# One bias row-add for each PSUM bank instead of one for each product, in a four-layer network on one core

## The chip, the cores and the metric

One Trainium2 chip, one core. The metric is the device time of one execution in microseconds (us), the median over the runs shown. Busy times, waits and the order of the work come from one profiled execution of the same program.

## What is computed

Four layers, each a feed-forward block, an attention block and the feed-forward block again, on x of shape (4, 512, 128) in float32. The parts that the change meets are the linear maps with a bias:

```python
q = (q_in @ Wq.T + bq)            # layer 1 feed-forward: k and v likewise
attn_out = ctx @ out_proj_w.T + out_proj_b
gates = softmax(x1 @ gate_w.T + gate_b)
logits = x @ router_w + router_b  # layer 2 feed-forward
q = x @ Wq.T + bq                 # layer 3 attention: k, v likewise, out with bo
x = x + h @ w2 + b2               # layer 3 feed-forward, two sub-layers
```

## The kernel before

The core works on one batch element at a time: 512 tokens are four tiles of 128 (NT = 4), a feature row is 128 wide. A unit is one block (for example layer 1's feed-forward) for one batch element, and has three parts: pre (normalization, projections, transposes), core (attention scores, softmax, weighing, or the experts) and post (out-projection, gates, the residual). In one slot the core of one unit, the pre of the next and the post of the one before are woven into one instruction order for each engine. That order is fixed by hand-set strings (ORDERS, line 2515): a letter names a stream and a number how many of its steps come next, a step being what stands between two yields. The engines then run their own queues in order and wait for each other at semaphores.

Pre and post each work in a lane: one PSUM bank (128 partitions by 512 float32) that TensorE fills and that ScalarE or VectorE empties; `lane.filled` and `lane.taken` count the two. TensorE waits for `lane.taken` ahead of each fill. TensorE's queue also holds 1180 matmuls that fill gaps (fillers, line 263), at fixed places of the order.

A bias is added on TensorE. `add_row` (line 294) multiplies a 3-row stationary tile of ones with the bias, which is held as three bfloat16 rows whose sum is the float32 value, and accumulates into the bank. A float32 product runs as two passes, each a weight load and a matmul; the row is one pass of bfloat16. The places:

- `project_heads` (line 406), for each of the four tiles, 384 columns for q, k and v out of the normalized and transposed input. With one source (layer 3's attention) this is one product and one row of 384 columns. Layer 1's feed-forward has two sources: a product and a row of 256 columns, then a product and a row of 128 columns. ScalarE empties the tile with three copies (lines 428 to 432).
- `out_project` (line 685): four products of 128 columns into one bank, a row behind each; VectorE adds the bank to the residual (line 713). The out-projections of layers 0 and 2 have no bias.
- `gates` (line 720): four products of 8 columns, a row behind each; VectorE reads them at line 746.
- `l3_layer_post` (line 2420): four tiles of 128 columns, each the sum of three products (the 341 hidden features in chunks of 128, 128 and 85), that is six passes, and a row behind each (line 2468). VectorE adds the bank at line 2493.
- Two places that the change leaves alone: the experts of layer 1 (line 1553, rows of 512 columns) and layer 1's attention (line 1614, rows of 16 columns).

Other lines named below: 529, ScalarE's copies of attention rows; 1121, 1126, 1157 and 1162, attention score matmuls and their masks; 1551, layer 1's expert products; 1221, VectorE's row maxima; 642, out-projections (layer 3's feed-forward among them) of four accumulating products for each tile, without a bias; 1806 and 1808, 8-column products without a bias; 2164, transposes in layer 3's feed-forward, which wait for VectorE's rotary work (line 2262).

Of the kernel before, what the change touches and what calls it, by code (L numbers as in the profile page):

```python
# [31 lines left out]
P = 128  # L32
B, L, D = 4, 512, 128
NT = L // P
# [3 lines left out]
NE = 8  # L38
# [258 lines left out]
    return nc.tensor.matmul(out, m.onesb[p:p + 3, :], m.rowparts[p:p + 3, at + a:at + b], start=False, stop=True, **kw)  # L297


def bank(m, i, n=512):  # L300
    return m.ps[:, i, 0:n]

# [103 lines left out]
def project_heads(nc, m, lane, a, srcs, row, q_dst, k_dst, V, q_scale, first_use=True):  # L406


    free = a.free
    f = lane.fills(NT)  # L410

    def tensor(pe):
        for t in range(NT):
            yield 2.0 * t
            if f + t > 0:
                pe.wait_ge(lane.taken, f + t)
            for src_T, weight, s, z in srcs:
                ins = nc.tensor.matmul(lane.at[:, s:z], src_T[:, t * P:(t + 1) * P], weight[:, s:z],  # L418
                                       start=True, stop=row is None)
                if row is not None:  # L420
                    ins = add_row(nc, m, lane.at[:, s:z], row, s, z)
            ins.then_inc(lane.filled, 1)

    def scalar(act):
        for t in range(NT):
            yield 2.0 * t + 1.0
            act.wait_ge(lane.filled, f + t + 1)
            nc.scalar.activation(q_dst[:, t, :], lane.at[:, 0:D], ACT.Copy, scale=q_scale)
            nc.scalar.copy(k_dst[:, t, :], lane.at[:, D:2 * D])
            if t == 0:  # L430
                free(act)
            nc.scalar.copy(v_heads(V)[:, t, :, 0:HD],
                           lane.at[:, 2 * D:3 * D].rearrange("p (h e) -> p h e", h=H)).then_inc(lane.taken, 1)

    def gpsimd(pool):
        yield 0.0
        if first_use:
            free(pool)
            nc.gpsimd.memset(v_heads(V)[:, :, :, HD:HD + 1], 1.0)
            nc.gpsimd.memset(V[:, :, 9 * H:VW], 0.0)  # L440

    lane.add(2.0 * NT + 0.5, tensor=tensor, scalar=scalar, gpsimd=gpsimd)
    return lane.taken, f + NT

# [240 lines left out]
def out_project(nc, m, lane, ot, oT, weight, row, dst, add, ready):  # L685
    f = lane.fills(2)

    def tensor(pe):
        yield 0.0
        pe.wait_ge(*ready)  # L690
        if f > 0:
            pe.wait_ge(lane.taken, f)
        for t in range(NT):
            ins = nc.tensor.transpose(lane.at[:, t * P:(t + 1) * P], ot[:, t, :], m.weight["ident"])
        ins.then_inc(lane.filled, 1)
        yield 2.0
        pe.wait_ge(lane.taken, f + 1)
        for t in range(NT):
            ins = nc.tensor.matmul(lane.at[:, t * P:(t + 1) * P], oT[:, t * P:(t + 1) * P], weight,
                                   start=True, stop=row is None)  # L700
            if row is not None:
                ins = add_row(nc, m, lane.at[:, t * P:(t + 1) * P], row)
        ins.then_inc(lane.filled, 1)

    def scalar(act):
        yield 1.0
        act.wait_ge(lane.filled, f + 1)
        nc.scalar.copy(oT, lane.at).then_inc(lane.taken, 1)

    def vector(dve):  # L710
        yield 4.0
        dve.wait_ge(lane.filled, f + 2)
        nc.vector.tensor_tensor(dst.rearrange("p t d -> p (t d)"), lane.at, add.rearrange("p t d -> p (t d)"),
                                ALU.add).then_inc(lane.taken, 1)

    lane.add(5.0, tensor=tensor, scalar=scalar, vector=vector)
    return lane.taken, f + 2


def gates(nc, m, lane, src_T, weight, row, k, keep_probability, sel):  # L720

    w = lane.w
    f = lane.fills(1)
    shifted, exped, gate_step, chosen = lane.note("shifted"), lane.note("exped"), lane.note("gate_step"), lane.note("chosen")
    lg = lane.at[:, 0:NT * NE].rearrange("p (t e) -> p t e", t=NT)
    full = [P, NT, NE]
    wide = [P, NT, NE, NE]

    def tensor(pe):
        yield 0.0  # L730
        pe.wait_ge(lane.taken, f)
        for t in range(NT):
            nc.tensor.matmul(lg[:, t, :], src_T[:, t * P:(t + 1) * P], weight, start=True, stop=False)
            ins = add_row(nc, m, lg[:, t, :], row)
        ins.then_inc(lane.filled, 1)

    def scalar(act):
        yield 2.5
        act.wait_ge(lane.taken, f + 1)
        nc.scalar.activation(w.gp[:, :, :], w.gl[:, :, :], ACT.Exp).then_inc(exped, 1)  # L740

    def vector(dve):
        n = Count()
        yield 1.5
        dve.wait_ge(lane.filled, f + 1)
        nc.vector.tensor_reduce(w.g4[:, 0:NT], lg, AX.X, ALU.max).then_inc(gate_step, 1)
        dve.wait_ge(gate_step, n.up())
        nc.vector.tensor_tensor(w.gl[:, :, :], lg, w.g4[:, 0:NT].unsqueeze(2).to_broadcast(full),
                                ALU.subtract).then_inc(lane.taken, 1)
        yield 3.5  # L750
        dve.wait_ge(exped, 1)
        nc.vector.tensor_reduce(w.g4[:, NT:2 * NT], w.gp[:, :, :], AX.X, ALU.add).then_inc(gate_step, 1)
        dve.wait_ge(gate_step, n.up())
        nc.vector.reciprocal(w.g4[:, 2 * NT:3 * NT], w.g4[:, NT:2 * NT]).then_inc(gate_step, 1)
        dve.wait_ge(gate_step, n.up())
        nc.vector.tensor_tensor(w.gl[:, :, :], w.gp[:, :, :],
                                w.g4[:, 2 * NT:3 * NT].unsqueeze(2).to_broadcast(full), ALU.mult).then_inc(gate_step, 1)
        yield 4.5
        dve.wait_ge(gate_step, n.up())
        other, own = w.gl[:, :, :].unsqueeze(2).to_broadcast(wide), w.gl[:, :, :].unsqueeze(3).to_broadcast(wide)  # L760
        nc.vector.tensor_tensor(w.cmp[:, 0], other, own, ALU.is_gt).then_inc(gate_step, 1)
        nc.vector.tensor_tensor(w.cmp[:, 1], other, own, ALU.is_equal).then_inc(gate_step, 1)
        yield 5.5
        dve.wait_ge(gate_step, n.up(2))
        tri8 = m.weight["tri8"].unsqueeze(1).to_broadcast([P, NT, NE * NE])
        nc.vector.tensor_tensor(w.cmp[:, 1].rearrange("p t a b -> p t (a b)"),
                                w.cmp[:, 1].rearrange("p t a b -> p t (a b)"), tri8, ALU.mult).then_inc(gate_step, 1)
        yield 6.0
        dve.wait_ge(gate_step, n.up())
        nc.vector.tensor_tensor(w.cmp[:, 0], w.cmp[:, 0], w.cmp[:, 1], ALU.add).then_inc(gate_step, 1)  # L770
        yield 6.5
        dve.wait_ge(gate_step, n.up())
        nc.vector.tensor_reduce(w.grank[:, :, :], w.cmp[:, 0], AX.X, ALU.add).then_inc(gate_step, 1)
        yield 7.0
        dve.wait_ge(gate_step, n.up())
        if keep_probability:
            nc.vector.scalar_tensor_tensor(out=sel, in0=w.grank[:, :, :], scalar=float(k), in1=w.gl[:, :, :],
                                           op0=ALU.is_lt, op1=ALU.mult).then_inc(chosen, 1)
        else:
            nc.vector.tensor_scalar(sel, w.grank[:, :, :], float(k), None, ALU.is_lt).then_inc(chosen, 1)  # L780

    lane.add(7.5, tensor=tensor, scalar=scalar, vector=vector)
    return chosen, 1

# [1635 lines left out]
def l3_layer_post(nc, m, lane, a, b, l):  # L2420
    s = m.post
# [27 lines left out]
    w2 = m.weight["l3f_w2"].rearrange("p (l c d) -> p l c d", l=DEPTH, c=NC3)  # L2449
# [4 lines left out]
    def tensor(pe):  # L2454
        for i in range(2 * NC3):
            yield 2.2 * i + (1.5 if i >= NC3 else 0.0)
            s_, c = (1, i) if i < NC3 else (0, i - NC3)
            at = s_ * HID3 + c * P
            pe.wait_ge(lane.taken, f + i)
            nc.tensor.matmul(lane.at[0:size[c], :], w1[:, l, at:at + size[c]], s.hT[:, :], start=True,  # L2460
                             stop=True).then_inc(lane.filled, 1)
        yield 2.2 * 2 * NC3 + 2.0
        pe.wait_ge(lane.taken, f + 2 * NC3)
        for t in range(NT):
            for c in range(NC3):
                nc.tensor.matmul(lane.at[:, t * P:(t + 1) * P], s.gated[0:size[c], c, t * P:(t + 1) * P],
                                 w2[0:size[c], l, c, :], start=(c == 0), stop=False)
            ins = add_row(nc, m, lane.at[:, t * P:(t + 1) * P], "l3f_b2", l * D, (l + 1) * D)
        ins.then_inc(lane.filled, 1)

    def scalar(act):
# [913 lines left out]
```

## Time and profile before

| | |
|---|---|
| median of 3 runs | 3130.27 us (3128.41 to 3135.72) |
| the profiled execution, span from first to last instruction | 3123.3 us |
| its time outside the span | not told by the profile; the median lies 7.0 us above the span |
| TensorE matmul (PE) busy | 2749.7 us, 88% |
| TensorE weight load (PEld) busy | 1757.8 us, 56% |
| VectorE (DVE) busy | 2224.2 us, 71% |
| ScalarE (ACT) busy | 1703.5 us, 55% |
| GpSimd (POOL) busy | 794.2 us, 25% |

The busy time of an engine is the union of its instructions' durations. Matmuls overlap in the array, so that the sum of their durations says more than the queue pays; the distance between two starts is what one of them takes from the queue. The chain is the work that ended last, followed back from the last instruction: at each step to whatever released it.

### The profile page before, as it was taken

Reading aid. Unit: us, or ns where it says so; the run is one execution under the profiler, and the core shown is the slowest. Engines: PE = TensorE matmul, PEld = TensorE weight load, DVE = VectorE, ACT = ScalarE, POOL = GpSimd, SP = SyncE. Lnnn points to the kernel's source line nnn. Section 1 sums busy time; section 2 is a strip of 40 time slices with the busy share of each in tenths; the row PEclk is TensorE's granted clock in tenths of the full one; section 3 lists DMA queues with packets and bytes.
Section 4 is the critical chain, followed back from the end, with each engine's and each line's share of the span. In section 5 each row is a group of like instructions: output and inputs, shape, how many; then the busy total and the mean of one; then the engine's idle time right before and its main releaser. Section 6 shows DMA issues by size and latency. Waiting matters only on the chain.

```text
span 3123.3 us, 66472 instructions
## 1 busy us (share of the span) xinstructions
PE 2749.7 (88%) x25741; PEld 1757.8 (56%) x25741; DVE 2224.2 (71%) x5316; ACT 1703.5 (55%) x4158; POOL 794.2 (25%) x809
## 2 busy tenths in 40 slices
PE   6878898899998899998878998999998889899998
PEld 3556665544455544467745887565653332455665
DVE  4766567788877677765566446889787777788884
ACT  2344533656622466543466434767765566767773
POOL 1010001111112111111232114646431112555550
PEclk8889997999999999998999989999999888999999
DMA  3523310000000000037500565010100000101001
GB/s 108 226 46 69 71 42 1 1 1 1 1 1 1 1 1 1 14 133 275 206 6 4 189 236 172 15 28 15 26 17 3 1 1 1 25 16 26 17 18 26
DMA packets 134803, 159.51 MB, mean 51 GB/s; under 512 B 82901, under 2 KB 109781, under 8 KB 132954
## 3 DMA queue, kind: packets, MB, share of 16 engines
q1 hardware_dynamic: 131962, 150.08, 15.7%
q8 instruction: 205, 3.36, 0.4%
q0 software_dynamic: 2048, 4.20, 0.4%
q10 hardware_dynamic: 480, 0.98, 0.1%
q14 instruction: 108, 0.88, 0.1%
HBM read 106.53 MB, written 30.61 MB: 44 GB/s over the span
## 4 chain that ended last, share of the span: by engine, by line
PE 47%; DVE 24%; ACT 10%; issue 8%; POOL 4%; DMA 3%; SPq 0%; DVEq 0%; POOLq 0%; ACTq 0%; another core or an unknown queue 0%
DVE nm L1221 5%; PE ps L1180 3%; PE ps L1955 3%; PE ps L1121 3%; PE ps L1157 3%; PE ps L565 3%; ACT hand L529 3%; PE ps L2157 3%; PE ps L418 2%; PE ps L2323 2%; PE ps L642 2%; DVE pre L2243 2%; PE ps L297 2%; PE ps L263 2%; PE ps L1551 1%
## 5 line engine op out<-in xcount | busy, mean ns | idle before, releaser
L1221 DVE TENSOR_REDUCE nm<-ps 128x2 f32<-128x256 f32 (+2 forms) x704 | 424.5, 637 | 87.1 <-PE ps L1121 50.1
L1270 ACT ACTIVATE core<-ps 128x512 f32<-128x512 f32 x672 | 359.1, 590 | 93.9 <-PE ps L1162 59.1
L359 POOL TENSOR_TENSOR rstd<-ve,weights 128x4 f32<-128x4 f32 x80 | 83.2, 1040 | 941.7 <-DVE ve L336 878.5
L2229 POOL TENSOR_TENSOR pre<-pre,sin 128x512 f32<-128x512 f32 x128 | 234.8, 1854 | 226.3 <-ACT pre L2200 199.6
L1121 PE MATMUL ps<-hand 128*128 128x128 bf16 (+4 forms) x1024 | 246.2, 315 | 44.0 <-DVE nm L1221 39.2
L529 ACT COPY hand<-ps 64x512 bf16<-64x512 bf16 x336 | 195.2, 581 | 126.7 <-PE ps L565 77.6
L1157 PE MATMUL ps<-hand 128*128 128x128 bf16 (+4 forms) x1024 | 223.0, 305 | 14.6 <-ACT hand L529 9.2
L2363 ACT ACTIVATE core<-ps,nm 128x128 f32<-128x128 f32 x512 | 182.5, 381 | 62.8 <-DVE nm L2380 62.0
L2234 POOL TENSOR_TENSOR ss<-ss,weights 128x16 f32<-128x16 f32 x64 | 195.9, 3061 | 71.0 <-DVE ss L2249 69.2
L2157 PE MATMUL ps<-weights,pre 128*128 128x512 f32 x384 | 203.2, 632 | 7.6 <-ACT pre L2203 4.5
L263 PE MATMUL ps<-identb 128*128 128x256 bf16 x1180 | 182.3, 283 | 18.3 <-PEq L3008 14.0
L1180 PE MATMUL ps<-core,hand 128*32 128x512 f32 (+3 forms) x2048 | 180.4, 447 | 8.3 <-ACT otok L1253 4.3
L1231 POOL CAST hand<-nm 128x16 bf16<-128x16 f32 x192 | 58.1, 303 | 501.4 <-DVE nm L1221 493.2
L1121 PEld LDWEIGHTS ps<-hand 128*128 128x128 bf16 (+1 forms) x1024 | 85.3, 98 | 158.7 <-DVE nm L1221 111.3
L1157 PEld LDWEIGHTS ps<-hand 128*128 128x128 bf16 (+1 forms) x1024 | 79.4, 97 | 159.6 <-ACT core L1270 91.1
L1955 PE MATMUL ps<-hand 128*128 128x128 f32 x1152 | 157.5, 296 | 1.2 <-DMA hand<-in_experts 1.2
L1955 PEld LDWEIGHTS ps<-hand 128*128 128x128 f32 x1152 | 151.1, 212 | 6.4 <-issue 3.4
L1971 ACT ACTIVATE core<-ps,hand 128x128 f32<-128x128 f32 x288 | 82.3, 370 | 125.3 <-PE ps L1955 122.1
L263 PEld LDWEIGHTS ps<-identb 128*128 128x128 bf16 x1180 | 111.9, 101 | 50.7 <-issue 32.8
L2323 PE MATMUL ps<-hand 64*64 64x128 f32 (+1 forms) x2048 | 134.6, 271 | 0.0
L1989 DVE SCALAR_TENSOR_TENSOR core<-ps,hand,core 128x128 f32<-128x128 f32 x288 | 81.1, 344 | 70.7 <-ACT core L1971 62.0
L565 PE MATMUL ps<-identb,hand 128*128 128x128 bf16 x768 | 78.7, 227 | 57.0 <-ACT hand L577 18.2
(348 smaller groups left out, 6693.3 us busy)
## 6 DMA issues: line engine op xcount, KB each, us to landing
hand<-in_experts SPq DMA_DIRECT2D x72, 836.0 KB, 6.7
shear<-post SPq DMA_DIRECT2D x64, 256.0 KB
core<-in_experts SPq DMA_DIRECT2D x16, 836.0 KB, 8.0
core<-shear SPq DMA_DIRECT2D x128, 64.0 KB, 2.2
hand<-hand SPq DMA_DIRECT2D x16, 512.0 KB, 4.4
hand<-hand SPq DMA_DIRECT2D x16, 384.0 KB, 5.6
pre<-sorted_in SPq DMA_DIRECT2D x8, 704.0 KB, 5.1
sorted_out<-core SPq DMA_DIRECT2D x88, 64.0 KB
```

What stands on the lines that cost most here:

```text
L263: nc.tensor.matmul(out, m.identb, m.identb.unsqueeze(1).to_broadcast([P, FILL // P, P]), start=True, stop=True)
L529: ins = copy(a.QX[64 * e:64 * e + 64, q_slot(2 * pair + e), :], src[64 * e:64 * e + 64, :])
L1121: ins = nc.tensor.matmul(b[:, n * nk:(n + 1) * nk], q[:, qt * P:(qt + 1) * P], k[:, lo:lo + nk], start=kind != BLOCK32 and n == 0, stop=Tr ...
L1157: ins = nc.tensor.matmul(b[:, n * w:(n + 1) * w], k[:, kt * P:(kt + 1) * P], q[:, s:z], start=kind != BLOCK32 and n == 0, stop=True, skip_ ...
L1180: ins = nc.tensor.matmul(m.ps[32 * j:32 * j + 32, OUT, s:z], a.V[:, kt, 9 * h:9 * h + 32], prob8[:, i % PROBS, n * w:(n + 1) * w], start=( ...
L1221: nc.vector.tensor_reduce(nm_of(unit), src, AX.X, ALU.max, negate=True).then_inc(negmax, 1)
L1270: nc.scalar.activation(prob8[:, i % PROBS, 0:w], m.ps[:, RING[at % NR], 0:w], ACT.Exp).then_inc(ring_out, 1)
L1955: ins = nc.tensor.matmul(m.ps[:, 2 * (i % 2) + s, c * P:(c + 1) * P], w1(i, s, c), a.xs[:, i * P:(i + 1) * P], start=True, stop=True)
L2157: nc.tensor.matmul(banks[at % N], s.hT[:, t * P:(t + 1) * P], qkv[:, l, i, :], start=True, stop=True).then_inc(lane.filled, 1)
L2229: ins = nc.gpsimd.tensor_tensor(o[:, :, :, z:z + hl], x[:, :, :, y0:y0 + hl], sn[:, t, :, z:z + hl].unsqueeze(2).to_broadcast([P, 2, LH, h ...
L2234: nc.gpsimd.tensor_tensor(m.ss[:, 1, 0:2 * LH], m.ss[:, 0, 0:2 * LH], m.weight["half"][:, 0:2 * LH], ALU.pow).then_inc(rooted, 1)
L2323: ins = nc.tensor.matmul(out[rows, r * P + at:(r + 1) * P], a.Q3[rows, c, n * WIN:(n + 1) * WIN], a.K3[rows, c, lo:(n + 1) * WIN], start=F ...
```

## The change

The row is added once for a whole bank or tile. The first product into the bank carries `start`, which marks the whole bank as fresh; the others no longer do, and overwrite because their columns have not been written since. The row comes last. Where four products share the same bias of n columns, the new `add_row_to_all` reads the row four times over (a stride of zero) and adds it to all 4 x n columns. `project_heads` adds one row over all columns of the tile.

```diff
+def add_row_to_all(nc, m, out, name, a=0, b=None):
+
+    p, at, n = m.row_at[name]
+    n = (n if b is None else b) - a
+    row = m.rowparts[p:p + 3, at + a:at + a + n].unsqueeze(1).to_broadcast([3, NT, n])
+    return nc.tensor.matmul(out.rearrange("p (t n) -> p t n", t=NT), m.onesb[p:p + 3, :], row, start=False, stop=True,
+                            skip_group_check=True)
...
             for src_T, weight, s, z in srcs:
                 ins = nc.tensor.matmul(lane.at[:, s:z], src_T[:, t * P:(t + 1) * P], weight[:, s:z],
-                                       start=True, stop=row is None)
-                if row is not None:
-                    ins = add_row(nc, m, lane.at[:, s:z], row, s, z)
+                                       start=s == 0, stop=True, skip_group_check=s > 0)
+            if row is not None:
+                ins = add_row(nc, m, lane.at[:, 0:srcs[-1][3]], row, 0, srcs[-1][3], skip_group_check=True)
             ins.then_inc(lane.filled, 1)
...
             ins = nc.tensor.matmul(lane.at[:, t * P:(t + 1) * P], oT[:, t * P:(t + 1) * P], weight,
-                                   start=True, stop=row is None)
-            if row is not None:
-                ins = add_row(nc, m, lane.at[:, t * P:(t + 1) * P], row)
+                                   start=t == 0, stop=True, skip_group_check=t > 0)
+        if row is not None:
+            ins = add_row_to_all(nc, m, lane.at, row)
         ins.then_inc(lane.filled, 1)
...
         for t in range(NT):
-            nc.tensor.matmul(lg[:, t, :], src_T[:, t * P:(t + 1) * P], weight, start=True, stop=False)
-            ins = add_row(nc, m, lg[:, t, :], row)
+            nc.tensor.matmul(lg[:, t, :], src_T[:, t * P:(t + 1) * P], weight, start=t == 0, stop=True,
+                             skip_group_check=t > 0)
+        ins = add_row_to_all(nc, m, lane.at[:, 0:NT * NE], row)
         ins.then_inc(lane.filled, 1)
...
                 nc.tensor.matmul(lane.at[:, t * P:(t + 1) * P], s.gated[0:size[c], c, t * P:(t + 1) * P],
-                                 w2[0:size[c], l, c, :], start=(c == 0), stop=False)
-            ins = add_row(nc, m, lane.at[:, t * P:(t + 1) * P], "l3f_b2", l * D, (l + 1) * D)
+                                 w2[0:size[c], l, c, :], start=(t == 0 and c == 0), stop=True,
+                                 skip_group_check=t + c > 0)
+        ins = add_row_to_all(nc, m, lane.at, "l3f_b2", l * D, (l + 1) * D)
         ins.then_inc(lane.filled, 1)
```

## Rows read from the trace of the kernel before

**Rows 1.** The page's busy times: us, share of the span, instructions of each engine.

```profile
PE 2749.7 (88%) x25741; PEld 1757.8 (56%) x25741; DVE 2224.2 (71%) x5316; ACT 1703.5 (55%) x4158; POOL 794.2 (25%) x809
```

**Rows 2.** The page's chain that ended last: shares by engine, then by line.

```profile
PE 47%; DVE 24%; ACT 10%; issue 8%; POOL 4%; DMA 3%; SPq 0%; DVEq 0%; POOLq 0%; ACTq 0%; another core or an unknown queue 0%
DVE nm L1221 5%; PE ps L1180 3%; PE ps L1955 3%; PE ps L1121 3%; PE ps L1157 3%; PE ps L565 3%; ACT hand L529 3%; PE ps L2157 3%; PE ps L418 2%; PE ps L2323 2%; PE ps L642 2%; DVE pre L2243 2%; PE ps L297 2%; PE ps L263 2%; PE ps L1551 1%
```

**Rows 3.** The list of cores: span and mean granted TensorE clock.

```profile
core 0: 3123.3 us, clock 0.946
```

**Rows 4.** Groups by line, all row-adds: busy us, mean ns | idle us before.

```profile
L297 PE MATMUL ps<-rowparts,onesb 3*128 3x128 bf16 (+5 forms) x336 | 86.4, 257 | 0.0
```

**Rows 5.** Timeline, an out_project bank: start us, us, instruction, count [idle before <-releaser].

```profile
634.66 0.49 PE L699 MATMUL ps<-weights,post 128*128 128x128 f32 x2
...
635.09 0.23 PE L297 MATMUL ps<-rowparts,onesb 3*128 3x128 bf16 x1
...
635.24 0.49 PE L699 MATMUL ps<-weights,post 128*128 128x128 f32 x2
```

**Rows 6.** Timeline, float32 products without a row: 128 columns, then 8 columns.

```profile
2150.52 1.06 PE L642 MATMUL ps<-weights,otok 128*128 128x128 f32 x8
...
2151.41 0.60 PE L2112 MATMUL ps<-weights,y 128*128 128x128 f32 x4
...
1295.25 0.81 PE L1806 MATMUL ps<-sel,weights 128*128 128x8 f32 x6
1295.92 0.37 PE L1808 MATMUL ps<-sel,weights 128*128 128x8 f32 x2
```

**Rows 7.** Timeline, layer 3's second feed-forward matmul: one tile to the next.

```profile
2145.56 0.94 PE L2466 MATMUL ps<-weights,post 128*128 128x128 f32 x6
...
2146.59 0.93 PE L2466 MATMUL ps<-weights,post 128*128 128x128 f32 x6
```

**Rows 8.** Timeline: a row of 512 columns, then one of 256 in project_heads.

```profile
653.28 0.38 PE L297 MATMUL ps<-rowparts,onesb 3*128 3x512 bf16 x1
653.60 0.39 PE L1157 MATMUL ps<-hand 128*128 128x512 bf16 x1
...
585.01 0.28 PE L297 MATMUL ps<-rowparts,onesb 3*128 3x256 bf16 x1
...
585.22 0.49 PE L418 MATMUL ps<-weights,pre 128*128 128x128 f32 x2
```

**Rows 9.** Timeline, a gates bank: two products and the row between them.

```profile
647.00 0.39 PE L733 MATMUL ps<-weights,post 128*128 128x8 f32 x2
...
647.32 0.17 PE L297 MATMUL ps<-rowparts,onesb 3*128 3x8 bf16 x1
647.42 0.30 PEld L733 LDWEIGHTS ps<-weights,post 128*128 128x128 f32 x2
```

**Rows 10.** Timeline, what waits next behind six banks, in the prediction's order.

```profile
585.90 0.28 ACT L428 ACTIVATE pre<-ps 128x128 f32<-128x128 f32 x1 [1.71 <-PE ps L297]
...
636.54 0.10 PEld L1157 LDWEIGHTS ps<-hand 128*128 128x128 bf16 x1 [0.21 <-ACT hand L529]
...
798.85 0.69 DVE L713 TENSOR_TENSOR y<-ps,y 128x512 f32<-128x512 f32 x1 [0.65 <-PE ps L297]
...
649.03 0.56 DVE L1221 TENSOR_REDUCE nm<-ps 128x1 f32<-128x384 f32 x1 [0.23 <-PE ps L1126]
...
2785.14 1.09 PE L2164 MATMUL ps<-weights,pre 128*128 128x128 f32 x8 [0.90 <-DVE pre L2262]
...
3119.16 0.69 DVE L2493 TENSOR_TENSOR y<-ps,y 128x512 f32<-128x512 f32 x1 [4.25 <-PE ps L297]
```

## The prediction

> **What bounds the kernel now.** I read the busy times first. TensorE is busy for 88% of the span [rows 1], so it is the first suspect, but busy time alone does not say what a shorter TensorE queue is worth. So the second view is the chain that ended last, and there the reader should see two things [rows 2]. TensorE holds 47% of the chain and VectorE 24%: the end is set by a relay between engines, TensorE running in it for about half the time. And the row-adds themselves, line 297, stand in the list with 2%. As 2% is rounded, that is at least 1.5%, or 47 us of the 3123.3 us span. Third, all row-adds together [rows 4]: 336 matmuls, never an idle moment ahead of them, so their cost is queue time and nothing else. How they get that cost is seen only in the order of time, where the distance from one start to the next, not the duration of one (durations overlap), is what the queue pays.
>
> **What the change removes.** Counted from the code: out_project has 12 banks with a row (8 of layer 1's feed-forward, 4 of layer 3's attention) and goes from four adds to one in each; the gates have 16 banks (8 and 8) and do the same; layer 3's second feed-forward matmul has 16 banks and does the same; project_heads with two sources (layer 1's feed-forward, 32 tiles) goes from two adds to one. Layer 3's project_heads has one source and keeps its 16 adds. So 36 + 48 + 48 + 32 = 164 of the 336 matmuls go, each with its weight load. No other engine's instruction, no DMA and no semaphore wait is added or removed; the order of the queues stays, since every step still yields as often as before.
>
> **What one add costs.** In an out_project bank the products begin 0.58 us apart (634.66 to 635.24), of which the row holds the queue for 0.15 us (635.09 to 635.24) and the two-pass product 0.43 us [rows 5]. The same two passes without a row between them: eight passes of such a shape run from 2150.52 to 2151.41, 0.111 us each, so 0.22 us a product [rows 6]. Hence a row costs its 0.15 us and another 0.21 us in its neighbours, paid once for each change between the 128-row products and the 3-row add. A row of 512 columns holds the queue for 0.32 us (653.28 to 653.60), one of 256 for 0.21 us (585.01 to 585.22) [rows 8]; from 0.15, 0.21 and 0.32 a row is about 0.10 us fixed and 0.42 ns a column.
>
> The Trainium skill's page "TensorE: Matmul & The Clock Gate", section "Back-to-back issue gap", gives an isolated matmul a gap of N / 2.4 + 2.5 ns: four rows of 128 columns would cost 223 ns, one of 512 columns 216 ns, and by that sum the change is worth some 7 ns a bank, so nothing. The rows above disagree: 0.15 and 0.32 us, and the slower product beside them.
>
> **The sum on TensorE's queue.** Each line keeps one change of shape and its 0.21 us, where it applies:
> - out_project: before 4 x 0.58 = 2.32; after 4 x 0.22 + 0.21 + 0.32 = 1.41 us. Saved 0.90 us x 12 = 10.8 us.
> - layer 3's second feed-forward matmul: a product of six passes and its row take 1.03 us (2145.56 to 2146.59) [rows 7], six passes without a row 6 x 0.111 = 0.67. Before 4.1, after 4 x 0.67 + 0.20 + 0.32 = 3.2 us. Saved 0.90 x 16 = 14.4 us.
> - gates: a product and its row take 0.42 us, the row 0.10 of it [rows 9]; six passes of the same 128x8 form without a row take 0.67 us, so 0.22 a product [rows 6], which leaves 0.10 for the change of shape. The new row has 32 columns, by the straight line above 0.12. Before 1.69, after 4 x 0.22 + 0.10 + 0.12 = 1.10 us. Saved 0.59 x 16 = 9.4 us.
> - project_heads with two sources: the 256-column row (0.21) and one change of shape (0.20) go, and the last row grows from 128 to 384 columns (+0.11). Saved 0.30 x 32 = 9.6 us. The row that is moved behind the second product was waited for by nobody: the semaphore stood on the tile's last instruction before and does after.
>
> Together 44 us of TensorE time. Three prices are not seen in the trace. A row that reads its 128 columns four times over: between the 0.32 us of a plain 512-column row and four rows by themselves, 0.62; a gain below 0.32 is excluded, since the columns are the same. I take 0.32, nearest by shape; the other end takes back 0.30 x 28 = 8 us. The gates' row lies between the 8-column 0.10 and the 128-column 0.15, at most 0.8 us in all. Products that start without clearing their bank: the passes of [rows 6] include accumulating ones at the same 0.111, so nothing, either way.
>
> **What of it reaches the end.** Two readings. The upper one: by count and length the rows hold the queue for 144 x 0.15 + 64 x 0.10 + 32 x 0.21 + 16 x 0.26 + 64 x 0.32 + 16 x 0.11 = 61 us (128, 8, 256, 384, 512 and 16 columns; those of 384 and 16 by the line above), and at least 47 us of that lies on the chain: 77%. So 0.77 x 44 = 34 us, if nothing else is late next. The lower one: I followed six banks to the next instruction that had to wait [rows 10], asking what was due next. At 585.80 a tile of project_heads ends and ScalarE has been idle 1.71 us for it: its 0.30 us survives. At 636.54, behind an out_project bank, TensorE is idle 0.21 us until ScalarE's copies end: none of its 0.90 survives. At 798.85 VectorE has been idle 0.65 us for the bank: 0.65 of 0.90. At 649.03, behind a gates bank, VectorE was idle 0.23: about 0.2 of 0.59. At 2785.14 TensorE waits 0.90 us for VectorE's rotary work: none of 0.90. At 3119.16 the last bank ends the program with VectorE idle 4.25: all 0.90. By kind, all of 9.6, 0.65 of 1.80 of 10.8, 0.2 of 0.59 of 9.4 and half of 14.4 us make 24 us. What is late next is thus ScalarE's copies or VectorE's maxima in the attention stages and the rotary chain in layer 3. Between 24 and 34 I take 25 us, by the lower reading: six banks are few, but the chain counts first arrivals only and so flatters.
>
> The profiled span less 25 is 3098 us; the span lies 7.0 us under the median of the runs, 3130.27, which has the time around the program in it, and 25 us off that is **3105 us**.
>
> **The rivals.** A measurement of this kernel can tell about 0.2%, 6.3 us, from no change.
> - *More than the chain says.* Where the row-adds are off the chain, an earlier bank may still let TensorE reach the chain's next product sooner. For it: no idle time ahead of any row [rows 4], so the queue is full wherever they stand. Against it: two of the six banks. Between 34 and 44 us, so about 3091 us. Chance 0.15.
> - *Absorbed.* The banks are at most 0.9 us each and the chain changes hands all the time, so the second-latest input may be close behind everywhere, as at 636.54 and 2785.14. For it: VectorE's 24% of the chain. Against it: the last bank, and 2% of the chain in line 297. Only a tenth survives: 5 us, 3125 us. Chance 0.13.
> - *A row costs only its columns.* If the fixed part of a row were hidden by the neighbours' weight loads, four rows of 128 would cost what one of 512 does and the change would not do what it says: 3130 us. The 0.58 against 0.22 + 0.15 speaks against it [rows 5, 6]. Chance 0.05. The rule of the Trainium skill's "TensorE: Matmul & The Clock Gate" above would have it so; the trace does not bear it out.
> - *Slower: the clock.* The one mechanism that can lose more than it gives is TensorE's granted clock, 0.946 in the mean [rows 3], so 0.108 of the span, 337 us, is at the lower of its two levels, 1.2 instead of 2.4 GHz. Less work on TensorE means more idle time between attention steps. A microsecond more at the low level costs about half of TensorE's 47% of the chain, 0.235 us. It decides from where it eats 25 us: 106 us more at the low level, a mean clock of 0.929; at 0.920 it costs 162 x 0.235 = 38 us, which gives 3143 us. Against it: the 25 us are under 1% of the span. Chance 0.07. The Trainium skill, "TensorE: Matmul & The Clock Gate", section "What's actually happening", states that the clock is low by default and that activity releases it; no run here shows yet which way it goes.
>
> **How the numbers follow.** The forecast has 0.60 and is wholly on the faster side. Of the absorbed case 0.05 is over 6.3 us and 0.08 within. Faster 0.60 + 0.15 + 0.05 = 0.80; same 0.08 + 0.05 = 0.13; slower 0.07. The range goes from 3094, just past the whole chain share (3130 - 34 = 3096), to 3126, which takes in the dearer broadcast row (25 less 6) and the absorbed case; outside stay half of the first rival, the clock and part of the no-change cases.
>
> **What would show it.** In the changed kernel's profile: 172 row-adds; products of an out_project bank about 0.22 us apart, with one row of about 0.32 us at the end; a six-pass product each 0.67 us; TensorE's busy time down by some tens of microseconds; VectorE's and ScalarE's counts as before. The chain's share of the row-adds should fall by about half. I am wrong in the prices if the products stay 0.43 us apart or the broadcast row takes 0.6; wrong in the chain if TensorE's queue loses 44 us and the span less than 10; and it is the clock if the mean falls under 0.93.

## The result, and the profile after

The changed kernel takes 3085.03 us (median of 4 runs, 3078.86 to 3098.45) against 3129.34 us (3119.28 to 3135.72) for the kernel before: ratio 0.9868 [0.9838, 0.9899], that is about 41 us less. The forecast was 3105 us with a range from 3094 to 3126. The direction was right, the size too small, and the time lies outside the range.

The changed kernel's page (busy times, then the shares of the chain by engine) and its list of cores answer to [rows 1 to 3]:

```profile
PE 2693.3 (88%) x25577; PEld 1731.7 (56%) x25577; DVE 2223.1 (72%) x5316; ACT 1702.4 (55%) x4158; POOL 794.7 (26%) x809
...
PE 45%; DVE 25%; ACT 10%; issue 7%; POOL 5%; DMA 3%; SPq 0%; POOLq 0%; DVEq 0%; ACTq 0%; PEld 0%; PEldq 0%
```

```profile
core 0: 3077.0 us, clock 0.951
```

TensorE has 164 matmuls fewer, as forecast; VectorE's and ScalarE's instruction counts are unchanged, their busy times nearly so; TensorE's share of the chain fell from 47% to 45%. The row-adds by line, as in [rows 4] (busy us, mean ns | idle us before): 128 + 44 = 172.

```profile
L297 PE MATMUL ps<-rowparts,onesb 3*128 3x512 bf16 (+2 forms) x128 | 44.2, 346 | 0.0
L305 PE MATMUL ps<-rowparts,onesb 3*128 3x512 bf16 (+1 forms) x44 | 14.0, 317 | 0.0
```

The timeline of the changed kernel, in the order of time: the out_project bank of [rows 5] and the wait behind it [rows 10]; a gates bank and the project_heads tile behind it, and an experts' row of 512 columns further on; a bank of layer 3's second feed-forward matmul; the last bank of the program.

```profile
633.47 1.11 PE L708 MATMUL ps<-weights,post 128*128 128x128 f32 x8
634.51 0.39 PE L305 MATMUL ps<-rowparts,onesb 3*128 3x512 bf16 x1
635.87 0.39 PE L1167 MATMUL ps<-hand 128*128 128x512 bf16 x1 [0.97 <-ACT hand L538]
...
722.39 1.06 PE L742 MATMUL ps<-weights,post 128*128 128x8 f32 x8 [0.18 <-ACT post L383]
723.38 0.18 PE L305 MATMUL ps<-rowparts,onesb 3*128 3x32 bf16 x1
723.49 0.92 PE L427 MATMUL ps<-weights,pre 128*128 128x256 f32 x4
724.35 0.33 PE L297 MATMUL ps<-rowparts,onesb 3*128 3x384 bf16 x1
724.61 0.39 PE L1167 MATMUL ps<-hand 128*128 128x512 bf16 x1
...
729.46 0.39 PE L297 MATMUL ps<-rowparts,onesb 3*128 3x512 bf16 x1
...
2108.98 2.94 PE L2476 MATMUL ps<-weights,post 128*128 128x128 f32 x24 [0.40 <-DVE post L2498]
2111.86 0.38 PE L305 MATMUL ps<-rowparts,onesb 3*128 3x512 bf16 x1
2112.17 0.66 PE L2174 MATMUL ps<-weights,pre 128*128 128x128 f32 x4
...
3069.62 2.94 PE L2476 MATMUL ps<-weights,post 128*128 128x128 f32 x24
3072.50 0.39 PE L305 MATMUL ps<-rowparts,onesb 3*128 3x512 bf16 x1
3072.92 0.69 DVE L2504 TENSOR_TENSOR y<-ps,y 128x512 f32<-128x512 f32 x1 [3.35 <-PE ps L305]
```

Read the distances between starts. The gates bank holds the queue for 1.10 us (722.39 to 723.49), as forecast to the hundredth; the layer 3 bank for 3.19 (2108.98 to 2112.17), forecast 3.2; the project_heads tile for 1.12 (723.49 to 724.61), where before the same kind took 1.42 (584.38 to 585.80). Two of the six readings of [rows 10] show here as well: behind the out_project bank TensorE's idle time grew from 0.21 to 0.97 us, so that most of the 0.90 that the bank saved was lost waiting for ScalarE, and at the last bank VectorE's wait fell from 4.25 to 3.35, all of the 0.90.

So the queue did what was forecast. What the sum left out shows in another view, the busy times by stretch. The first fence is the kernel before, the second the changed one, each a stretch up to a gates bank and the stretch behind that same bank (us, busy us and count of PE, PEld, DVE, ACT, POOL, then the granted clock PEclk, the DMA share, GB/s):

```profile
719.00:727.00 8.00, 7.79 (x55) 4.71 (x53) 4.98 (x11) 4.83 (x13) 0.95 (x1) 1.00 0.00 0
727.00:734.00 7.00, 7.00 (x35) 3.05 (x34) 3.76 (x12) 1.92 (x6) 0.00 (x0) 0.51 0.01 2
```

```profile
716.00:723.50 7.50, 6.99 (x53) 4.46 (x51) 5.43 (x16) 5.15 (x14) 1.01 (x1) 1.00 0.00 0
723.50:731.00 7.50, 7.43 (x51) 3.71 (x50) 6.13 (x19) 3.85 (x12) 0.61 (x1) 1.00 0.01 2
```

Behind the bank the kernel before runs 7 us at a granted clock of 0.51, nearly all at 1.2 GHz; the changed kernel runs on at 2.4 GHz. And TensorE was not idle before the fall: by the profile it was busy for 7.79 of 8.00 us, a larger share than in the changed kernel (6.99 of 7.50), where the clock did not fall.

### The profile page after: what moved, and what is told of

Its sections match the earlier page's. It is cut to its first block, busy times and chain, and to the rows that moved or that the text cites. A ratio compares the mean times of both kernels' runs of the same rounds, so it can differ in the third digit from the quotient of the medians.

```text
span 3077.0 us, 66144 instructions
## 1 busy us (share of the span) xinstructions
PE 2693.3 (88%) x25577; PEld 1731.7 (56%) x25577; DVE 2223.1 (72%) x5316; ACT 1702.4 (55%) x4158; POOL 794.7 (26%) x809
## 4 chain that ended last, share of the span: by engine, by line
PE 45%; DVE 25%; ACT 10%; issue 7%; POOL 5%; DMA 3%; SPq 0%; POOLq 0%; DVEq 0%; ACTq 0%; PEld 0%; PEldq 0%
DVE nm L1231 6%; PE ps L1190 3%; PE ps L1965 3%; ACT hand L538 3%; PE ps L574 3%; PE ps L1167 3%; PE ps L1131 3%; PE ps L2167 2%; PE ps L2333 2%; PE ps L651 2%; PE ps L427 2%; DVE pre L2253 2%; POOL ss L2244 2%; PE ps L1950 2%; PE ps L263 1%
## 5 line engine op out<-in xcount | busy, mean ns | idle before, releaser
L1965 PEld LDWEIGHTS ps<-hand 128*128 128x128 f32 x1152 | 144.9, 204 | 5.0 <-issue 2.8
L2333 PEld LDWEIGHTS ps<-hand 64*64 64x64 f32 x2048 | 103.4, 134 | 45.1 <-issue 45.1
```

Of the source, the lines that this page charges most:

```text
L1965: ins = nc.tensor.matmul(m.ps[:, 2 * (i % 2) + s, c * P:(c + 1) * P], w1(i, s, c), a.xs[:, i * P:(i + 1) * P], start=True, stop=True)
L2333: ins = nc.tensor.matmul(out[rows, r * P + at:(r + 1) * P], a.Q3[rows, c, n * WIN:(n + 1) * WIN], a.K3[rows, c, lo:(n + 1) * WIN], start=F ...
```

## The experiments

Three explanations of the missing 20 us were to be told apart: the queue's prices or their survival were undersized; the clock rose and gave the rest; or the first runs differed by chance. To hold queue and clock apart, every execution's time at the low level is worked out as 2 x (1 - granted clock) x span, and one straight line is laid through all executions of all runs, with one slope for all and a constant for each kernel: a microsecond at the low level goes with 0.33 ± 0.013 us of span (one standard error, as with every ± here; residual 2.8 us). The four executions of the changed kernel show it by themselves: spans of 3077.0, 3088.0, 3078.4 and 3096.7 us at 0.951, 0.945, 0.948 and 0.942; from the first to the last that is 301 to 359 us at the low level, and 19.7 us for 58, 0.34. The last column is the difference of two constants: against the kernel before at equal time at the low level. It rests on that line, and on executions of several chips together (on four of them the kernel before had medians from 3124.6 to 3129.6 us); the ratios compare runs on one chip.

| run | kernel | ratio [95%] | mean clock | us at the low level | mean span against before, us | of it at equal low level, us |
|---|---|---|---|---|---|---|
| (71 executions) | before | 1 | 0.941 | 367 | 0 | 0 |
| first result | changed | 0.9868 [0.9838, 0.9899] | 0.9465 | 330 | -42.1 | -30.0 ± 1.5 |
| e1 | before again | 0.9996 [0.998, 1.0012] | 0.941 | 370 | +0.6 | -0.2 ± 0.9 |
| e2 | changed again | 0.9870 [0.9848, 0.9892] | 0.945 | 341 | -37.8 | -29.2 ± 1.3 |
| e3 | changed, queue time given back | 0.9929 [0.9906, 0.9952] | 0.9485 | 320 | -20.9 | -5.5 ± 1.4 |
| e4 | four adds, all behind the products | 0.9882 [0.9859, 0.9905] | 0.9445 | 343 | -35.8 | -28.0 ± 1.2 |
| e5 | project_heads alone | 0.9960 [0.9943, 0.9978] | 0.943 | 356 | -13.2 | -9.6 ± 0.9 |
| e6 | out_project alone | 0.9993 [0.9977, 1.0009] | 0.940 | 374 | -2.9 | -5.3 ± 0.9 |
| e7 | gates alone | 0.9920 [0.990, 0.994] | 0.9485 | 320 | -24.1 | -8.6 ± 1.4 |
| e8 | layer 3's second matmul alone | 0.9966 [0.9946, 0.9987] | 0.9405 | 371 | -7.4 | -8.8 ± 0.9 |
| e9 | changed, rows of full height | 0.9798 [0.9773, 0.9824] | 0.949 | 311 | -64.6 | -46.3 ± 1.4 |
| e10 | before, rows of full height | 0.9808 [0.9783, 0.9834] | 0.9495 | 310 | -61.1 | -42.3 ± 1.4 |
| e11 | all but the gates | 0.9914 [0.9892, 0.9935] | 0.944 | 348 | -29.6 | -23.4 ± 1.2 |
| e12 | before, gates filled | 0.9955 [0.994, 0.997] | 0.947 | 328 | -16.3 | -3.4 ± 1.1 |

**The two kernels again.** No edit.

> The kernel before, unchanged, to see its mean granted clock in several executions. Theory Q (queue): the change took 44 us from TensorE's queue and nothing else; of it 25 to 34 us reach the end, and the rest of the measured 41 us is a higher clock by chance, so the clocks of this run and of the changed kernel have the same mean over the executions, 0.946. Theory C (clock): the clock of this one stays lower than the changed kernel's in the mean over the executions, by 0.003 or more, because the row-adds themselves hold it down. Time by both: ratio 1.00, about 3130 us.

> The changed kernel, unchanged, for its clock and time over more executions. Theory Q with chance: 3096 to 3105 us in the mean, clock 0.946 as in the kernel before. Theory C: 3085 us again, clock 0.949 or more in the mean.

Measured: 0.9996 and 0.9870. The gain is no chance of one run, and the clock is part of it again: 0.945 against 0.941. The changed kernel's 3091.16 us and its clock lie between the numbers of the two theories, and the clocks of the two kernels are not the same, as theory Q would have them.

**The queue time given back.** The changed kernel with as much TensorE time as it saved, as identity matmuls of 256 columns (0.109 us each) into the last 256 columns of the lane's bank, ahead of the products of each changed place (the first of these carries `start`): 3 for a tile of project_heads, 8 for an out_project bank, 5 for a gates bank, 8 for one of layer 3, 400 in all.

```diff
+def pad(nc, m, lane, n):
+    out = lane.at[:, L - FILL:L].rearrange("p (a b) -> p a b", b=P)
+    for _ in range(n):
+        nc.tensor.matmul(out, m.identb, m.identb.unsqueeze(1).to_broadcast([P, FILL // P, P]), start=True, stop=True)
...
         pe.wait_ge(lane.taken, f)
+        pad(nc, m, lane, 5)
         for t in range(NT):
             nc.tensor.matmul(lg[:, t, :], src_T[:, t * P:(t + 1) * P], weight, start=t == 0, stop=True,
```

> The changed kernel, with as much of TensorE's queue time given back as the sum says was taken, 400 identity matmuls of 256 columns (0.11 us each, 44 us) ahead of the same banks' products: 8, 8, 5 and 3 for an out_project bank, a bank of layer 3's second feed-forward matmul, a gates bank and a project_heads tile. They use the full array, unlike the 3-row adds. Theory Q: back at the time of the kernel before, 3125 to 3135 us. Theory C (the row-adds keep the clock down): the queue part is given back but not the clock part, so some 15 us remain, 3115 us, with a clock above the kernel before's. If the queue's sum was too small, a gain remains at an equal clock.

Measured: 0.9929 [0.9906, 0.9952], 3108.01 us. Its timeline at a gates bank and the project_heads tile behind it:

```profile
728.86 0.72 PE L303 MATMUL ps<-identb 128*128 128x256 bf16 x5 [0.18 <-ACT post L389]
...
730.42 0.50 PE L303 MATMUL ps<-identb 128*128 128x256 bf16 x3
...
731.77 0.39 PE L1178 MATMUL ps<-hand 128*128 128x512 bf16 x1
```

The queue is nearly as long as before: the bank takes 1.56 us (728.86 to 730.42) against 1.70 (725.36 to 727.06, shown below), the tile 1.35 against 1.42. Still the kernel is 0.7% faster, 20.9 us of span. At equal low level only 5.5 us are left, part of which is the queue time not quite given back; so the queue's part went, and the clock's part stayed and grew (0.9485). The two are separate gains.

**Order without fewer adds.** The changed kernel, but with the adds of a bank one by one behind its last product (336 adds again).

```diff
-        if row is not None:
-            ins = add_row_to_all(nc, m, lane.at, row)
+        if row is not None:
+            for t in range(NT):
+                ins = add_row(nc, m, lane.at[:, t * P:(t + 1) * P], row, skip_group_check=True)
```

> The changed kernel, but with one add for each product again, all of a bank's adds behind its last product. The number of row-adds is that of the kernel before, 336; the changes of shape between products and rows are those of the changed kernel. If a row's price is its neighbours' (changes of shape, 0.21 us) and its fixed part only an entry fee, this is within 10 us of the changed kernel, 3085 to 3100 us, rows of 128 columns 0.06 us apart. If each row has its fixed 0.10 us wherever it stands, three more rows cost 0.10 to 0.15 us each, 164 of them about 16 us of queue, and 10 us of it come back: 3095 to 3105 us.

Measured: 0.9882 [0.9859, 0.9905], 3094.58 us, as good as the change within the intervals (-28.0 against -29.2 and -30.0 us at equal low level). Its timeline at the same out_project bank:

```profile
633.43 1.11 PE L709 MATMUL ps<-weights,post 128*128 128x128 f32 x8
634.47 0.39 PE L297 MATMUL ps<-rowparts,onesb 3*128 3x128 bf16 x4
635.83 0.39 PE L1170 MATMUL ps<-hand 128*128 128x512 bf16 x1 [0.96 <-ACT hand L539]
```

Four adds of 128 columns behind each other are over in 0.39 us, like the one of 512. So it is not the number of adds that costs here, but each change between products and adds.

**One part at a time.** The hunks of the diff one by one: project_heads, out_project, the gates, layer 3's second feed-forward matmul; and all but the gates.

> Only project_heads changed (32 tiles, one row-add of 384 columns in place of two); queue time taken 9.6 us. By the prediction's lower reading all of it survives, 9.6 us at an equal clock; by the share of its adds on the chain 8.7 us. Theory C adds a clock part: where the tiles, the gates and the row-adds lie densest, 700 to 750 us from the start, the two profiles of the kernel before have 6.8 us at the low clock and the changed kernel none; if it is these tiles' adds that do it, 3 to 5 us more and a mean clock above 0.941. In all 9 to 14 us, 3116 to 3121 us.

> Only out_project changed (12 banks); queue time taken 10.8 us. Lower reading 3.9 us at an equal clock, chain share 6.3 us. Theory C: up to 3 us more from the clock. 3120 to 3126 us.

> Only the gates changed (16 banks); queue time taken 9.4 us. Lower reading 3.2 us at an equal clock, chain share 6.5 us. Theory C: some 3 us more from the clock, as some of these banks lie where the clock fell (727 us, 1840 us from the start). 3120 to 3126 us.

> Only layer 3's second feed-forward matmul changed (16 banks); queue time taken 14.4 us. Lower reading 7.2 us at an equal clock, chain share 11.7 us. Theory C: nothing from the clock, since in layer 3 the kernel before has hardly a low stretch beside these banks. 3118 to 3122 us.

> The change without its gates: project_heads, out_project and layer 3's second feed-forward matmul changed, the gates with a row-add behind each product as before. Theory G (the clock falls at the gates): the gates alone brought a mean clock of 0.949 and 8.8 us at an equal clock, so here the clock is back near 0.941 to 0.943 and low stretches begin at 4 or more of the 16 gates banks; 22 to 25 us off at an equal clock, 3103 to 3110 us. Rival (the clock gain belongs to the change as a whole, less TensorE time anywhere): a clock of 0.945, 3093 to 3098 us.

Measured: ratios 0.9960, 0.9993, 0.9920, 0.9966, and 0.9914 for the three without the gates. The times, 3113.42, 3126.75, 3104.67, 3122.89 and 3100.31 us, all miss what was expected of them, most by 1 to 3 us, the gates alone by 15 us on the fast side. The gates alone, 9.4 us of queue, bring nearly twice what any other part does (24.1 us of mean span, project_heads 13.2), and they are the part that lifts the clock: 47 us less at the low level (367 to 320), against 11 for project_heads and none for the other two. out_project alone cannot be told from no change, though at equal low level it gives its 5 us. The clock's parts do not simply add: without the gates 19 us less at the low level, with them (both runs of the changed kernel) 26 to 37, with the gates alone 47. So e11, whose clock of 0.944 lies between the 0.941 to 0.943 of theory G and the 0.945 of its rival, does not by itself decide between them.

Where does the clock fall? A program of 16 gates banks gives a count for each profile: in how many does a stretch at the low level begin between the bank's start and 5 us past its end. With the gates as before: 6 (before), 8 (e1), 7 (e8), 5 (e6), 5 (e11), 4 (e5). With the gates changed: 2 (changed), 2 (e2), 2 (e7), 2 (e4), 2 (e3). The stretches that begin there come to 17 to 58 us at the low level in each of the six profiles, 33 in the mean, and to 7 in each of the five. That is 26 of the 41 us by which the low time of the two groups differs (360 and 319 us in the mean); where the other 15 lie was not followed.

**Work added at the gates.** The kernel before with one identity matmul of 256 columns ahead of each product of 8 columns, 64 in all.

```diff
         for t in range(NT):
+            pad(nc, m, lane, 1)
             nc.tensor.matmul(lg[:, t, :], src_T[:, t * P:(t + 1) * P], weight, start=True, stop=False)
             ins = add_row(nc, m, lg[:, t, :], row)
```

> The kernel before, with one identity matmul of 256 columns over the full array ahead of each product of the gates, 64 in all: 7 us more of TensorE's queue and not a row-add less. If the clock falls at the gates because the array has next to nothing to do there for 1.7 us (theory G), the mean clock rises from 0.941 towards 0.945 to 0.949 and the added work is paid for or more: 3115 to 3128 us. If the clock falls there because of the row-adds or the bank's length, it stays at 0.941 and the time grows by the added queue, 3132 to 3136 us.

Measured: 0.9955 [0.994, 0.997], 3113.29 us, clock 0.947, 2 banks of 16 with a fall. Adding work to the busiest engine made the kernel faster. Its timeline at the same bank as above, then its windows:

```profile
729.16 0.28 PE L303 MATMUL ps<-identb 128*128 128x256 bf16 x1 [0.18 <-ACT post L380]
729.28 0.29 PE L740 MATMUL ps<-weights,post 128*128 128x8 f32 x2
729.50 0.17 PE L297 MATMUL ps<-rowparts,onesb 3*128 3x8 bf16 x1
729.60 0.28 PE L303 MATMUL ps<-identb 128*128 128x256 bf16 x1
...
730.94 0.70 PE L424 MATMUL ps<-weights,pre 128*128 128x256 f32 x2
...
737.51 0.39 PE L297 MATMUL ps<-rowparts,onesb 3*128 3x512 bf16 x1
```

```profile
723.00:731.00 8.00, 7.74 (x58) 4.90 (x58) 4.78 (x11) 4.63 (x13) 0.75 (x1) 1.00 0.00 0
731.00:738.00 7.00, 6.84 (x45) 3.21 (x46) 5.32 (x16) 2.92 (x10) 0.00 (x0) 1.00 0.01 2
```

And the kernel before at that place:

```profile
725.36 0.39 PE L733 MATMUL ps<-weights,post 128*128 128x8 f32 x2 [0.18 <-ACT post L374]
...
726.96 0.17 PE L297 MATMUL ps<-rowparts,onesb 3*128 3x8 bf16 x1
727.06 1.19 PE L418 MATMUL ps<-weights,pre 128*128 128x256 f32 x2
...
736.59 0.39 PE L297 MATMUL ps<-rowparts,onesb 3*128 3x512 bf16 x1
```

A product and its row with the filler in it take 0.44 us (729.16 to 729.60), 0.42 without [rows 9]: the filler is hidden almost wholly. From the project_heads tile behind the gates to the first experts' row the kernel before takes 9.53 us (727.06 to 736.59), the filled one 6.57 (730.94 to 737.51) with the same instructions: one fall of the clock, 6.9 us at the low level (0.98 of 7.00), cost 2.96 us here, 0.43 for each. The changed kernel takes 5.97 for that stretch (723.49 to 729.46): the filled one's 6.57 less 0.30 for each of its two project_heads tiles.

**No change of shape.** Both kernels with rows of full height: the add reads all 128 rows of the tile of biases, which holds three groups of three rows and zeros between them, and the stationary tile, 128 rows now, has ones at the three rows of the wanted bias and zeros elsewhere (one tile for each of the three groups). Setting these up costs seven VectorE instructions at the start.

```diff
-    return nc.tensor.matmul(out, m.onesb[p:p + 3, :], m.rowparts[p:p + 3, at + a:at + b], start=False, stop=True, **kw)
+    return nc.tensor.matmul(out, m.rowones[p // 32], m.rowparts[:, at + a:at + b], start=False, stop=True, **kw)
...
-    row = m.rowparts[p:p + 3, at + a:at + a + n].unsqueeze(1).to_broadcast([3, NT, n])
+    row = m.rowparts[:, at + a:at + a + n].unsqueeze(1).to_broadcast([P, NT, n])
```

> The changed kernel, but every row-add takes all 128 rows: the stationary tile has ones in the bias's three rows and zeros in the others, and the row tile is zero where no bias stands. The sum is the same; no row-add changes the shape any more. If the price of a row is the change of shape (0.10 us into it, 0.10 us out of it, and most of its own fixed 0.10 us), 172 adds lose about 0.3 us each, 50 us of queue, of which two thirds reach the end, and the clock rises again: 3050 to 3062 us. If the price is the row-add as an instruction, whatever its shape, nothing changes: 3085 to 3091 us.

> The kernel before, with all 336 adds where they were, one for each product, but over all 128 rows as in the run above. If the change of shape is what the row-adds cost, this alone is faster than the changed kernel: of the 336 adds each gives back about 0.25 to 0.3 us, some 90 us of queue, two thirds of it at the end, 3060 to 3070 us, with the clock above the changed kernel's. If what counts is the number of adds, it stays near the kernel before, 3115 to 3130 us.

Measured: 0.9798 [0.9773, 0.9824] on the changed kernel, 0.9808 [0.9783, 0.9834] on the kernel before with all its 336 adds in place. The intervals lie wholly below that of the change, 0.9868 [0.9838, 0.9899]: taking away the change of shape brings more than taking away adds, and it beats both kernels. It acts at more places, though: at all 336 adds, those of the experts and of layer 1's attention among them, where the change took away 164. The times, 3064.84 and 3068.27 us, are a little over and within what was expected. The timeline of e10, an out_project bank and a gates bank:

```profile
632.83 0.44 PE L699 MATMUL ps<-weights,post 128*128 128x128 f32 x2
633.11 0.22 PE L297 MATMUL ps<-rowparts,rowones 128*128 128x128 bf16 x1
633.17 0.44 PE L699 MATMUL ps<-weights,post 128*128 128x128 f32 x2
633.44 0.22 PE L297 MATMUL ps<-rowparts,rowones 128*128 128x128 bf16 x1
...
645.16 0.37 PE L733 MATMUL ps<-weights,post 128*128 128x8 f32 x2
645.38 0.17 PE L297 MATMUL ps<-rowparts,rowones 128*128 128x8 bf16 x1
645.40 0.37 PE L733 MATMUL ps<-weights,post 128*128 128x8 f32 x2
```

A product and its row take 0.34 us (632.83 to 633.17) in place of 0.58 [rows 5], and at the gates 0.24 (645.16 to 645.40) in place of 0.42 [rows 9], with the same number of instructions and columns. What is left of a row of 128 columns is about 0.11 us over the bare product's 0.22. One fall of the clock stands at the 16 gates banks, in e9 as in e10, though e10's banks have all the adds they had.

## Why the prediction was wrong in size

**The queue's prices: right.** A gates bank was forecast at 1.10 us and takes 1.10, a layer 3 bank at 3.2 and takes 3.19, a project_heads tile was to save 0.30 and saves 0.30. The change of shape between 128-row products and 3-row adds, 0.21 us, is confirmed by taking it away: 0.24 us less at an out_project product (0.58 to 0.34), 0.18 at a gates product, where 0.10 had been taken for it and another 0.10 for the row itself. The unknown broadcast row cost the lower end, 0.31 us (2111.86 to 2112.17). One reading of it was off: the fixed 0.10 us of a row belongs to the change of shape, not to the row, since four adds behind each other take as long as one (e4). It did not change the sum, because the change leaves one add behind the products anyway.

The Trainium skill, "TensorEngine Tiling (Array Packing)", section "Key Properties", states that changing the tiling mode drains TensorE. The traces of e4 (four adds behind each other in 0.39 us) and e10 (0.34 us in place of 0.58) agree in direction; the page gives no price, and that a 3-row stationary tile counts as another mode is not told by the profile.

**What reaches the end: about right.** 25 us were taken; at equal low level 29 to 30 are measured, inside the 24 to 34 of the two readings. Kind by kind, forecast against the run of that part alone: project_heads 9.6 and 9.6, out_project 3.9 and 5.3, layer 3 7.2 and 8.8, gates 3.2 and 8.6. The three without the gates come to 20.7 forecast and 23.4 measured together (e11). The gates' term is the one mis-sized by much: a single bank, that at 649.03, stood for sixteen. The traces narrow it down. VectorE's 5316 instructions come in the same order in both kernels, so that the time from the sixth ahead of the gates' first read (line 746) to the fifteenth behind it can be set side by side, before and e7. At the seven banks where neither run has the low clock, e7 takes 0.22, 0.00, 0.59, 0.60, 0.16, 0.59 and 0.59 us less, 0.39 in the mean; the fifth is unsure, as the two runs of the kernel before differ by 0.79 us there. The first of these is the bank that the prediction read, and it read it rightly; it was not typical. Sixteen times 0.39 is about 6 us, an estimate. The rest of the 8.6 can be clock: a microsecond at the low level behind a gates bank cost 0.43 where the line through all runs takes 0.33, and 47 us at 0.10 would be 4.7 us. The line's -3.4 for e12, whose queue is no shorter than the kernel before's, points the same way.

**The clock: the step that failed.** The queue alone would have given 3130 less 30, about 3100 us, inside the range; the clock took the time out of it. The prediction had the clock in one place, as the rival that loses: "Less work on TensorE means more idle time between attention steps." It gave a rise no chance and no price. The clock rose, from 0.941 to between 0.945 and 0.9465 in the mean of the runs, 26 to 37 us less at the low level, worth 9 to 12 us at 0.33 each. With 29 to 30 us from the queue that makes the 38 to 42 us measured in span. Two things in the step were wrong. Its direction: taking this work away did not lower the clock. TensorE was busy for 7.79 of the 8.00 us before it fell, with products of 8 columns and changes of shape among them; with most changes of shape gone (e7), all of them (e10), or full matmuls added beside them (e12), it falls at 1 or 2 gates banks of 16 in place of 4 to 8. The price too: half of TensorE's share of the chain gave 0.235 us for a microsecond at the low level, the runs give 0.33. And [rows 3] read 0.946 off one execution; over all its executions the kernel before has 0.941, so that there was more low time to win back than the profile showed. The 7.0 us between that execution's span and the median are not the time around the program either: a run's time is only about 1.8 us over its own span (3133.17 and 3131.4 us in e1).

The Trainium skill, "TensorE: Matmul & The Clock Gate", section "What's actually happening", states that activity releases the clock. e12 agrees, where added matmuls went with a clock of 0.947 in place of 0.941; the profile's busy share alone does not tell it, since the clock fell after 7.79 busy us of 8.00.

**The rivals.** More than the chain says gave about 3091 us, the nearest of the times, by a mechanism that did not happen: at equal low level 34 to 44 us were not reached. Absorbed is seen at single banks (0.21 to 0.97 us of idle time at the out_project bank) but not in the sum. A row costs only its columns holds for adds behind each other (e4) and nearly for rows of full height (e10), not for the kernel as it was. What would have shown the clock at fault, a mean under 0.93, did not come.

What stays open: what exactly at a gates bank lets the clock fall, the changes of shape, the 8-column products or both. e12 and e10 each make the falls rare in a different way; that the bank is long is not it, since e12's is longer still (1.78 us, 729.16 to 730.94, against 1.70).

## What to carry to other kernels

In this kernel a thin matmul between full ones was paid for mostly by the change of shape beside it, not by its columns. So count the changes, put thin ones behind each other, or pad the thin operand with zeros to the neighbours' height, which at all 336 adds was worth more here than halving their number. Before removing work from TensorE, find where in the trace its granted clock falls and what it was doing just before; a stretch with a high busy share can still be the one behind which the clock falls, and mending it is then a gain of its own. To price a part at under half a per cent, hold the clock apart from the queue with a line through many executions.

## What the runs showed that was not expected

- 64 matmuls added to an engine that is 88% busy made the kernel faster: 0.9955 [0.994, 0.997], with the clock falling at 2 gates banks of 16 in place of 6 to 8.
- The kernel before gains as much from zeros as from anything tried: 336 adds of 128 rows in place of 3 rows, 0.9808 [0.9783, 0.9834], with TensorE's busy time at 2667.4 us against 2749.7 [rows 1]. Its page (72 of its matmuls are missing from the trace; the weight loads, 25741, are all there):

```profile
PE 2667.4 (87%) x25669; PEld 1743.6 (57%) x25741; DVE 2222.3 (72%) x5323; ACT 1700.5 (55%) x4158; POOL 793.7 (26%) x809
```

- Once the shape stays the same, collecting the adds is worth little: e9 against e10 is -46.3 against -42.3 us at equal low level, each ± 1.4, and their ratios' intervals overlap.
